# Order of the gather matmuls and of the first weight load within the routed experts of a mixture-of-experts stage

## The chip, the cores and the metric

One Trainium2 chip, eight cores. The batch has eight sequences and each core computes one of them on its own; nothing is exchanged. The time is that of the slowest core in microseconds (us) on the device.

## What is computed

One transformer layer with adaptive layer norm: an attention block, then the feed-forward block below, each with a residual. Only the feed-forward block is touched.

```python
def _L0_ffn_ref(hidden_states, gate_w, sh_gate, sh_up, sh_down, rt_gate, rt_up, rt_down):
    ...
    x = hidden_states.reshape(-1, h)
    logits = x @ gate_w
    top_val = jnp.max(logits, axis=-1, keepdims=True)
    top_id = jnp.argmax(logits, axis=-1)
    score = jax.nn.sigmoid(top_val)
    xs = x * score
    g = jnp.einsum('th,ehi->eti', xs, rt_gate)
    u = jnp.einsum('th,ehi->eti', xs, rt_up)
    act = jax.nn.silu(g) * u
    y = jnp.einsum('eti,eih->eth', act, rt_down)
    onehot = jax.nn.one_hot(top_id, E, dtype=x.dtype)
    routed = jnp.einsum('eth,te->th', y, onehot)
    shared = _swiglu(x, sh_gate, sh_up, sh_down)
    return (shared + routed).reshape(b, s, h)
```

Per core there are 2048 tokens of width 1024, eight experts (E) and an inner width of 2048. Weights come as float32.

## The kernel before, in words

The kernel gives each token to its best expert alone. Up to 384 tokens (`CAP`, three blocks `NSC` of 128) go to each expert. Tokens are collected and put back by matmuls with 0/1 matrices: `Pg_buf` (scaled by the score) gathers, `Ps_buf` scatters.

Each expert e goes through these stages, all on the same engines in program order:

- **Gate and up** (from line 962): 16 steps over `ic`, chunks of 128 of the inner width. `load_guchunk` brings a chunk of `rtg` into `wg_ch[ic % 2]` and of `rtu` into `wu_ch[ic % 2]`, two buffers each, one step ahead. TensorE does 8 + 8 matmuls (line 175) on the gathered tokens `Xg`; ScalarE and VectorE turn them into `act_sl`.
- **Build** (line 993 on): `build_Ps(e)` (lines 917 to 937) makes the scatter matrix by TensorE, ScalarE and VectorE; then `build_Pg(e + 1)` (line 904) makes the next gather matrix by 16 VectorE instructions.
- **Down** (loop around line 1006): 16 steps over `ic`. `load_wd` brings 128 rows of `rtd` into `wd_bf[ic % 2]`, also two buffers; six matmuls add into the six banks pp[2] to pp[7]. In between stand the eight **gather units** of the next expert (`gather_unit(e + 1, dc)`, 16 matmuls of 128x384 of line 175 and one VectorE copy to `Xg`, line 951): one behind every second step. The last expert has none.
- **Yg** (line 1021): six VectorE copies of the six banks, behind any copy to `Xg` on that engine.
- **Scatter** (line 1036 ends it): 32 groups of three matmuls, each followed by one VectorE update of `Xf`.

All weight loads are issued by GpSimd (POOL) and cast to bf16 on the way. POOL works through its queue in program order; a load waits there until TensorE has read the buffer that it overwrites. The loads of chunk 0 of gate and up stand at the head of each expert (lines 960 and 961), chunk 1 right behind them. Nothing plans the order: it is the order in which the Python code emits, and `Emit.op` adds the waits that the buffers need.

Of the kernel before, what the change touches and what calls it, by code (L numbers as in the profile page):

```python
# [104 lines left out]
def build_nc(S=2048, NH=16, IDIM=2048, E=8, CAP=384, debug_stop=None):  # L105
# [3 lines left out]
    IC = IDIM // 128  # L109
# [6 lines left out]
    def din(name, shape, dtype=F32):  # L116
        return nc.dram_tensor(name, shape, dtype, kind="ExternalInput")
# [12 lines left out]
    rtg_h = din("rtg", [E, 2, DC, 128, IH])  # L130
    rtu_h = din("rtu", [E, 2, DC, 128, IH])
# [22 lines left out]
    with em.ctx:  # L154
        ctx = em.ctx

        def sbuf(name, shape, dtype=F32, stack=None):
            return (stack or ctx).enter_context(
                nc.sbuf_tensor(name, shape, dtype))
# [5 lines left out]
        def dma(dst_ap, src_ap, writes, reads=(), eng="sync", sem=None):  # L165
            assert sem is not None
            em.op(eng, lambda E, d=dst_ap, s=src_ap: E.dma_start(d, s),  # L167
                  reads=reads, writes=writes, sem=sem, delta=16)

        def mmg(chain, writes, reads):  # L170
            n = len(chain)
            for i, (o, l, r) in enumerate(chain):
                em.op("tensor",
                      lambda E, o=o, l=l, r=r, a=(i == 0), z=(i == n - 1):
                      E.matmul(o, l, r, start=a, stop=z,  # L175
                               skip_group_check=True),
                      reads=(reads if (i == 0 or i == n - 1) else ()),
                      writes=(writes if (i == 0 or i == n - 1) else ()))
# [511 lines left out]
        with ExitStack() as ph4:  # L690
# [19 lines left out]
            def router_tc(tc):  # L710
                for t4 in range(4):
                    tb = tc * 4 + t4
                    if tb >= NB:
# [42 lines left out]
            wg_ch = [sbuf(f"wg_ch{i}", [128, DC * 128], BF16, ph4)  # L756
                     for i in range(2)]
            wu_ch = [sbuf(f"wu_ch{i}", [128, DC * 128], BF16, ph4)
                     for i in range(2)]
            rwg = [Res(), Res()]  # L760
            rwu = [Res(), Res()]
# [58 lines left out]
            def load_guchunk(ppe, prouted, src, dst, rr, ic, csem):  # L820
                hf = ic // (IC // 2)
                cc = (ic % (IC // 2)) * 128
                ap = (src.ap()[ppe, hf] if prouted else src.ap()[hf])
                dma(dst[:].rearrange("p (c n) -> p c n", c=DC),
                    ap.rearrange("c p n -> p c n")[:, :, cc:cc + 128],
                    writes=[rr], eng="gpsimd", sem=csem)
# [74 lines left out]
            def build_Pg(e):  # L901
                for tb in range(NB):
                    em.op("vector",
                          lambda E_, t=tb, e=e, NE=E: E_.tensor_scalar(  # L904
                              Pg_buf[:, t * CAP:t * CAP + CAP],
                              iotaf[:, 0:CAP],
                              rank_f[:, t * NE + e:t * NE + e + 1],
                              score_f[:, t:t + 1],
                              ALU.is_equal, ALU.mult),
                          reads=[rrk, rscf, rconst], writes=[rPg])  # L910
# [46 lines left out]
            for dc in range(DC):  # L957
                gather_unit(0, dc)
            for e in range(E):
                load_guchunk(e, True, rtg_h, wg_ch[0], rwg[0], 0, "dwg0")  # L960
                load_guchunk(e, True, rtu_h, wu_ch[0], rwu[0], 0, "dwu0")
                for ic in range(IC):
                    cb_ = ic % 2
                    if ic + 1 < IC:
                        load_guchunk(e, True, rtg_h, wg_ch[(ic + 1) % 2],
                                     rwg[(ic + 1) % 2], ic + 1,
                                     f"dwg{(ic + 1) % 2}")
                        load_guchunk(e, True, rtu_h, wu_ch[(ic + 1) % 2],
                                     rwu[(ic + 1) % 2], ic + 1,
                                     f"dwu{(ic + 1) % 2}")  # L970
                    pg, pu = pp[2 + (ic % 2)], pp[4 + (ic % 2)]
                    rpg, rpu = rpp[2 + (ic % 2)], rpp[4 + (ic % 2)]
                    mmg([(pg[:, 0:CAP],
                          wg_ch[cb_][:, dc * 128:(dc + 1) * 128],
                          Xg[:, dc * CAP:(dc + 1) * CAP])
                         for dc in range(DC)],
                        writes=[rpg], reads=[rwg[cb_], rXg])
                    mmg([(pu[:, 0:CAP],
                          wu_ch[cb_][:, dc * 128:(dc + 1) * 128],
                          Xg[:, dc * CAP:(dc + 1) * CAP])  # L980
                         for dc in range(DC)],
                        writes=[rpu], reads=[rwu[cb_], rXg])
                    em.op("scalar",
                          lambda E, p=pg, i=ic: E.activation(  # L984
                              silu_sb[i % 2][:, 0:CAP], p[:, 0:CAP],
                              AF.Silu),
                          reads=[rpg], writes=[rsilu[ic % 2]])
                    em.op("vector",
                          lambda E, i=ic, p=pu: E.tensor_mul(  # L989
                              act_sl[:, i * 512:i * 512 + CAP],  # L990
                              silu_sb[i % 2][:, 0:CAP], p[:, 0:CAP]),
                          reads=[rsilu[ic % 2], rpu], writes=[ract])
                build_Ps(e)
                if e + 1 < E:
                    build_Pg(e + 1)
                gu = list(range(DC)) if e + 1 < E else []
                gui = 0
                for ic in range(IC):
                    load_wd(e, True, rtd_h, ic)
                    for sc in range(NSC):  # L1000
                        for dh in range(2):
                            k = sc * 2 + dh
                            em.op("tensor",
                                  lambda E, i=ic, s2=sc, d2=dh, b2=ic % 2,
                                  k=k, a=(ic == 0), z=(ic == IC - 1):
                                  E.matmul(  # L1006
                                      pp[2 + k][:],
                                      act_sl[:, i * 512 + s2 * 128:
                                             i * 512 + (s2 + 1) * 128],
                                      wd_bf[b2][:, d2 * 512:(d2 + 1) * 512],  # L1010
                                      start=a, stop=z,
                                      skip_group_check=True),
                                  reads=[rwd[ic % 2], ract],
                                  writes=([rpp[2 + k]] if ic in (0, IC - 1)
                                          else ()))
                    while gui < len(gu) * (ic + 1) // IC:
                        gather_unit(e + 1, gu[gui])
                        gui += 1
                for k in range(NSC * 2):
                    em.op("vector",  # L1020
                          lambda E_, k=k: E_.tensor_copy(  # L1021
                              Yg[:, k * 512:(k + 1) * 512], pp[2 + k][:]),
                          reads=[rpp[2 + k]], writes=[rYg])
                for dc in range(DC):
                    for tc in range(NTC):
                        k = 6 + (dc * NTC + tc) % 2
                        chain = [(pp[k][:],
                                  Yg[:, sc * D + dc * 128:
                                     sc * D + (dc + 1) * 128],
                                  Ps_buf[:, (sc * NTC + tc) * 512:  # L1030
                                         (sc * NTC + tc + 1) * 512])
                                 for sc in range(NSC)]
                        mmg(chain, writes=[rpp[k]], reads=[rYg, rPs])
                        em.op("vector",
                              lambda E_, d=dc, t=tc, k=k:
                              E_.scalar_tensor_tensor(  # L1036
                                  Xf[d][:, t * 512:(t + 1) * 512],
                                  pp[k][:],
                                  mod_sb[:, GB + d:GB + d + 1],
                                  Xf[d][:, t * 512:(t + 1) * 512],  # L1040
                                  ALU.mult, ALU.add),
                              reads=[rpp[k], rmod, rXf[dc]],
                              writes=[rXf[dc]])
# [90 lines left out]
```

How the kernel before makes its waits and increments, by code:

```python
        def run(E, fn=fn, final=tuple(final), sem=sem, delta=delta):  # L71
            for (s, v) in final:
                E.wait_ge(sems[s], v)
            ins = fn(E)
            ins.then_inc(sems[sem], delta)
            return ins
# [28 lines left out]
def build_nc(S=2048, NH=16, IDIM=2048, E=8, CAP=384, debug_stop=None):  # L105
# [299 lines left out]
        def _dump_and_exit(aps_res):  # L405
            rout = Res()
            for (dst, src, rr, eng) in aps_res:
                dma(dst, src, writes=[rout], reads=[rr], eng=eng, sem="so")
            fin = em.cnt["so"]
            em.raw("sync", lambda E: E.wait_ge(em.sems["so"], fin))
            em.flush()
# [629 lines left out]
                                  ALU.mult, ALU.add),  # L1041
                              reads=[rpp[k], rmod, rXf[dc]],
                              writes=[rXf[dc]])
            em.flush()
        rout = Res()
        for dc in range(DC):
            dma(y_h.ap()[dc * 128:(dc + 1) * 128, :], Xf[dc][:],
                writes=[rout], reads=[rXf[dc]], sem="so")
        fin = em.cnt["so"]
        em.raw("sync", lambda E: E.wait_ge(em.sems["so"], fin))
        em.flush()
    return nc
```

## Time and profile before

| | us |
|---|---|
| median of 2 runs | 3915.04 (3908.28 to 3921.79) |
| profiled execution | 3910.82 |
| its span on the slowest core (core 3) | 3909.3 |
| spans of the eight cores | 3862.2 to 3909.3 |
| TensorE busy in that span | 2721.3 (70%) |

The profiled execution is 1.5 us longer than its span, and 4.2 us below the median. The profile gives for each engine its instructions with start and duration, and for each idle time what ended it (the releaser). TensorE's instructions are pipelined, so the distance between starts tells more than the durations.

### The profile page before, as it was taken

Reading aid. Unit: us, or ns where it says so; the run is one execution under the profiler, and the core shown is the slowest. Engines: PE = TensorE matmul, PEld = TensorE weight load, DVE = VectorE, ACT = ScalarE, POOL = GpSimd, SP = SyncE. Lnnn points to the kernel's source line nnn. Section 1 sums busy time; section 2 is a strip of 40 time slices with the busy share of each in tenths; the row PEclk is TensorE's granted clock in tenths of the full one; section 3 lists DMA queues with packets and bytes.
Section 4 is the critical chain, followed back from the end, with each engine's and each line's share of the span. In section 5 each row is a group of like instructions: output and inputs, shape, how many; then the busy total and the mean of one; then the engine's idle time right before and its main releaser. Section 6 shows DMA issues by size and latency. Waiting matters only on the chain.

```text
span 3909.3 us, 36235 instructions; the slowest of 8 cores (3862.2 to 3909.3 us)
## 1 busy us (share of the span) xinstructions
PE 2721.3 (70%) x11400; PEld 1135.4 (29%) x11400; DVE 970.3 (25%) x1892; ACT 630.9 (16%) x1007; POOL 468.1 (12%) x614
## 2 busy tenths in 40 slices
PE   2972888888788888617767756676666767675854
PEld 2950322222222222203222323232222222232321
DVE  0024221221221211451110132233232423232312
ACT  0032233333333332321000000000001010100000
POOL 0000000000000000003222312121212121212120
PEclk9985877878887865858999979898989889898987
DMA  4402300000000000009979937483838383838483
GB/s 156 161 33 18 34 6 3 9 3 6 9 3 1 1 1 0 1 1 100 99 85 99 103 44 73 57 81 49 81 49 81 49 81 49 82 48 86 51 90 108
DMA packets 466446, 204.25 MB, mean 52 GB/s; under 512 B 438231, under 2 KB 438490, under 8 KB 463194
## 3 DMA queue, kind: packets, MB, share of 16 engines
q0 software_dynamic: 462368, 184.60, 41.1%
q1 hardware_dynamic: 3898, 17.32, 1.3%
q8 instruction: 104, 1.70, 0.2%
q14 instruction: 76, 0.62, 0.1%
HBM read 352.89 MB, written 8.39 MB: 92 GB/s over the span
## 4 chain that ended last, share of the span: by engine, by line
DMA 22%; PE 19%; DVE 7%; issue 5%; ACT 0%; DVEq 0%; POOL 0%; POOLq 0%; ACTq 0%
PE pp L175 12%; DMA wu_ch<-rtu 7%; DMA wd_bf<-rtd 6%; DMA wd_bf<-shd 4%; DMA wu_ch<-shu 3%; PE pp L1006 3%; PE pp L869 2%; DVE Xf L1036 2%; DVE Ps_buf L937 2%; DMA wg_ch<-rtg 2%; DVE Pg_buf L904 2%; DMA wg_ch<-shg 1%; DVE Yg L1021 1%; PE pp L917 1%; PE pp L930 0%
## 5 line engine op out<-in xcount | busy, mean ns | idle before, releaser
L550 PE MATMUL s_ps<-Qall,Kall 64*128 64x512 bf16 (+3 forms) x640 | 256.1, 414 | 122.7 <-DVE s_ps L559 94.0
L593 PE MATMUL z_ps<-PT,Vb 128*64 128x512 bf16 (+3 forms) x640 | 284.3, 444 | 58.9 <-ACT PT L567 40.9
L984 ACT ACTIVATE silu<-pp 128x384 f32<-128x384 f32 x128 | 62.9, 491 | 1392.0 <-PE pp L175 1392.0
L175 PE MATMUL pp<-Ps_buf,Yg 128*128 128x512 bf16 x768 | 235.3, 404 | 67.5 <-DVE Yg L1021 41.0
L605 PE MATMUL l_ps<-PT,onescol_s 128*1 128x512 bf16 (+3 forms) x640 | 263.8, 412 | 0.0
L175 PE MATMUL pp<-Xg,wu_ch 128*128 128x384 bf16 x1024 | 195.5, 335 | 96.3 <-DMA wu_ch<-rtu 95.2
L1006 PE MATMUL pp<-wd_bf,act_sl 128*128 128x512 bf16 x768 | 204.7, 411 | 74.9 <-DMA wd_bf<-rtd 74.4
L175 PE MATMUL pp<-Xg,wg_ch 128*128 128x384 bf16 x1024 | 194.9, 335 | 70.8 <-DMA wg_ch<-rtg 69.0
L175 PE MATMUL pp<-Pg_buf,h2tm 128*128 128x384 bf16 x1024 | 191.6, 345 | 61.2 <-DVE Pg_buf L904 61.2
L567 ACT ACTIVATE PT<-s_ps 128x1024 bf16<-128x1024 f32 x192 | 191.2, 1013 | 231.9 <-PE s_ps L550 230.5
L244 PE MATMUL mod_ps<-c_sil,wmodb 128*128 128x1 f32 x768 | 164.0, 352 | 76.2 <-ACT c_sil L225 76.2
L1036 DVE SCALAR_TENSOR_TENSOR Xf<-pp,mod_sb,Xf 128x512 f32<-128x512 f32 x256 | 192.0, 751 | 78.5 <-PE pp L175 70.2
L869 PE MATMUL pp<-act_sl,wd_bf 128*128 128x512 bf16 x512 | 132.9, 410 | 98.9 <-DMA wd_bf<-shd 97.8
L989 DVE TENSOR_TENSOR act_sl<-silu,pp 128x384 bf16<-128x384 f32 x128 | 70.9, 554 | 474.9 <-PE pp L175 444.3
L244 PEld LDWEIGHTS mod_ps<-c_sil,wmodb 128*128 128x128 f32 x768 | 163.9, 333 | 76.2 <-issue 76.2
L167 POOL DMA_DIRECT2D wg_ch<-rtg x128 | 112.4, 878 | 521.1 <-PE pp L175 503.2
L577 ACT ACTIVATE PT<-s_ps 128x512 bf16<-128x512 f32 (+3 forms) x256 | 110.5, 437 | 300.1 <-DVE s_ps L559 208.3
L175 PEld LDWEIGHTS pp<-Xg,wu_ch 128*128 128x128 bf16 x1024 | 95.2, 99 | 191.6 <-issue 141.4
L550 PEld LDWEIGHTS s_ps<-Qall,Kall 64*128 64x128 bf16 x640 | 60.0, 95 | 301.0 <-issue 290.3
L175 PEld LDWEIGHTS pp<-Pg_buf,h2tm 128*128 128x128 bf16 x1024 | 104.6, 103 | 145.9 <-issue 81.6
L175 PE MATMUL pp<-Hb,wu_ch 128*128 128x512 bf16 x512 | 122.9, 383 | 31.5 <-DMA wu_ch<-shu 31.0
L175 PEld LDWEIGHTS pp<-Xg,wg_ch 128*128 128x128 bf16 x1024 | 95.2, 99 | 164.3 <-issue 114.4
(142 smaller groups left out, 2608.8 us busy)
## 6 DMA issues: line engine op xcount, KB each, us to landing
wg_ch<-rtg POOLq DMA_DIRECT2D x128, 256.0 KB, 6.3
wu_ch<-rtu POOLq DMA_DIRECT2D x128, 256.0 KB, 6.5
wd_bf<-rtd POOLq DMA_DIRECT2D x128, 256.0 KB, 4.2
wmodb<-wmod POOLq DMA_DIRECT2D x8, 3072.0 KB, 13.2
wg_ch<-shg POOLq DMA_DIRECT2D x64, 256.0 KB, 6.3
wu_ch<-shu POOLq DMA_DIRECT2D x64, 256.0 KB, 6.2
wd_bf<-shd POOLq DMA_DIRECT2D x64, 256.0 KB, 4.1
Xf<-x SPq DMA_DIRECT2D x8, 1024.0 KB
```

The costliest lines, as they stand in the source:

```text
L167: em.op(eng, lambda E, d=dst_ap, s=src_ap: E.dma_start(d, s), reads=reads, writes=writes, sem=sem, delta=16)
L175: E.matmul(o, l, r, start=a, stop=z, skip_group_check=True),
L244: lambda E, b=b, j=j, dc=dc: E.matmul(mod_ps[:, j:j + 1], wmod_bf[b][:, j * 128:(j + 1) * 128], c_sil[:, dc:dc + 1], start=(dc == 0 and j ...
L550: E.matmul(p[:, o + c:o + 512], Kall[bb][h, k * 128:(k + 1) * 128], Qall[bb][h, q], start=True, stop=True, skip_group_check=True),
L567: lambda E, p=sb_, t=pt: E.activation(t[:, 0:1024], p[:, 0:1024], AF.Exp),
L577: E.activation(t[:, o + c:o + 512], p[:, o + c:o + 512], AF.Exp),
L593: E.matmul(z_ps[zz, c:512], Vb[bb][:, k * 128 + h * 64: k * 128 + h * 64 + 64], t[:, o + c:o + 512], start=a, stop=z, skip_group_check=True),
L605: E.matmul(l_ps[:, c:512], onescol[:], t[:, o + c:o + 512], start=a, stop=z, skip_group_check=True),
L869: E.matmul(pp[d][:], wd_bf[b2][:, d * 128:(d + 1) * 128], act_sl[:, i * 512:(i + 1) * 512], start=a, stop=z, skip_group_check=True),
L904: lambda E_, t=tb, e=e, NE=E: E_.tensor_scalar(Pg_buf[:, t * CAP:t * CAP + CAP], iotaf[:, 0:CAP], rank_f[:, t * NE + e:t * NE + e + 1], sc ...
L1006: E.matmul(pp[2 + k][:], act_sl[:, i * 512 + s2 * 128: i * 512 + (s2 + 1) * 128], wd_bf[b2][:, d2 * 512:(d2 + 1) * 512], start=a, stop=z, ...
L1036: E_.scalar_tensor_tensor(Xf[d][:, t * 512:(t + 1) * 512], pp[k][:], mod_sb[:, GB + d:GB + d + 1], Xf[d][:, t * 512:(t + 1) * 512], ALU.mu ...
```

## The change

The gather units are emitted twice as densely: one behind each of the down steps 0 to 7, and none behind steps 8 to 15. The loads of chunk 0 of the next expert move from the head of that expert to behind down step 12, that is between the loads of down chunks 12 and 13. Chunk 1 stays where it was. Nothing is added or removed but by these moves; the last expert's down stage stays as it is.

```diff
@@ -957,8 +957,9 @@
             for dc in range(DC):
                 gather_unit(0, dc)
             for e in range(E):
-                load_guchunk(e, True, rtg_h, wg_ch[0], rwg[0], 0, "dwg0")
-                load_guchunk(e, True, rtu_h, wu_ch[0], rwu[0], 0, "dwu0")
+                if e == 0:
+                    load_guchunk(e, True, rtg_h, wg_ch[0], rwg[0], 0, "dwg0")
+                    load_guchunk(e, True, rtu_h, wu_ch[0], rwu[0], 0, "dwu0")
                 for ic in range(IC):
                     cb_ = ic % 2
                     if ic + 1 < IC:
@@ -1013,9 +1014,14 @@
                                   reads=[rwd[ic % 2], ract],
                                   writes=([rpp[2 + k]] if ic in (0, IC - 1)
                                           else ()))
-                    while gui < len(gu) * (ic + 1) // IC:
+                    while gui < min(len(gu), len(gu) * (ic + 1) * 2 // IC):
                         gather_unit(e + 1, gu[gui])
                         gui += 1
+                    if ic == IC - 4 and e + 1 < E:
+                        load_guchunk(e + 1, True, rtg_h, wg_ch[0], rwg[0],
+                                     0, "dwg0")
+                        load_guchunk(e + 1, True, rtu_h, wu_ch[0], rwu[0],
+                                     0, "dwu0")
```

On TensorE, the down stage of an expert (line 1006 is the down matmul; `pp<-Pg_buf,h2tm` is a gather unit; `pp<-Ps_buf,Yg` the scatter) reads before:

```order
L930 MATMUL pp<-rank_row,onesh_s 128x512 x4
L1006 MATMUL pp<-wd_bf,act_sl 128x512 x12
L175 MATMUL pp<-Pg_buf,h2tm 128x384 x16
L1006 MATMUL pp<-wd_bf,act_sl 128x512 x12
L175 MATMUL pp<-Pg_buf,h2tm 128x384 x16
```

and its end, before:

```order
L1006 MATMUL pp<-wd_bf,act_sl 128x512 x12
L175 MATMUL pp<-Pg_buf,h2tm 128x384 x16
L175 MATMUL pp<-Ps_buf,Yg 128x512 x96
```

The same stage of the changed kernel begins with (line 1006 is 1007 there):

```order
L930 MATMUL pp<-rank_row,onesh_s 128x512 x4
L1007 MATMUL pp<-wd_bf,act_sl 128x512 x6
L175 MATMUL pp<-Pg_buf,h2tm 128x384 x16
L1007 MATMUL pp<-wd_bf,act_sl 128x512 x6
L175 MATMUL pp<-Pg_buf,h2tm 128x384 x16
```

and ends with:

```order
L1007 MATMUL pp<-wd_bf,act_sl 128x512 x6
L175 MATMUL pp<-Pg_buf,h2tm 128x384 x16
L1007 MATMUL pp<-wd_bf,act_sl 128x512 x48
L175 MATMUL pp<-Ps_buf,Yg 128x512 x96
```

One down step (six matmuls) now stands ahead of the first gather unit where there were two, and eight down steps (48 matmuls) follow each other without a gather unit.

On POOL, the queue around the end of an expert before (each row is one load or a run of loads, `rtd` the down weights):

```order
L167 DMA wd_bf<-rtd 128x1024 x16
L167 DMA wg_ch<-rtg 128x8x128
L167 DMA wu_ch<-rtu 128x8x128
L167 DMA wg_ch<-rtg 128x8x128
L167 DMA wu_ch<-rtu 128x8x128
```

and now:

```order
L167 DMA wd_bf<-rtd 128x1024 x13
L167 DMA wg_ch<-rtg 128x8x128
L167 DMA wu_ch<-rtu 128x8x128
L167 DMA wd_bf<-rtd 128x1024 x3
L167 DMA wg_ch<-rtg 128x8x128
L167 DMA wu_ch<-rtu 128x8x128
```

The pair of chunk 0 has moved ahead of the last three down loads; the pair of chunk 1 still stands behind the last one.

## Rows read from the trace of the kernel before

**Rows 1.** The page's first line: the span of the profiled core and of all cores.

```profile
span 3909.3 us, 36235 instructions; the slowest of 8 cores (3862.2 to 3909.3 us)
```

**Rows 2.** Windows: stretch, us, busy us by engine (instructions), granted clock, DMA share, GB/s.

```profile
3620.40:3671.60 51.20, 38.31 (x197) 18.53 (x196) 8.52 (x14) 0.00 (x0) 9.88 (x16) 0.97 0.65 83
...
3704.00:3769.50 65.50, 45.89 (x257) 22.97 (x255) 9.06 (x16) 7.86 (x16) 25.59 (x30) 1.00 1.27 121
...
3789.30:3842.80 53.50, 28.33 (x98) 9.37 (x98) 6.41 (x9) 0.00 (x0) 7.41 (x14) 0.85 0.51 69
```

**Rows 3.** Waits of TensorE from 2440 us on: total us, times, longest.

```profile
PE pp L1006 <- DMA wd_bf<-rtd: 74.4, 66, 3.1
```

**Rows 4.** Timeline of TensorE, down stage of expert 6: start, us, [idle before <-releaser].

```profile
3603.16 4.89 PE L1006 MATMUL pp<-wd_bf,act_sl 128*128 128x512 bf16 x12
3615.31 5.28 PE L175 MATMUL pp<-Pg_buf,h2tm 128*128 128x384 bf16 x16 [7.25 <-DVE Pg_buf L904]
3620.38 3.15 PE L1006 MATMUL pp<-wd_bf,act_sl 128*128 128x512 bf16 x12
...
3629.20 1.46 PE L1006 MATMUL pp<-wd_bf,act_sl 128*128 128x512 bf16 x6 [1.11 <-DMA wd_bf<-rtd]
3630.50 2.76 PE L175 MATMUL pp<-Pg_buf,h2tm 128*128 128x384 bf16 x16
3633.10 1.46 PE L1006 MATMUL pp<-wd_bf,act_sl 128*128 128x512 bf16 x6
...
3663.41 2.76 PE L175 MATMUL pp<-Pg_buf,h2tm 128*128 128x384 bf16 x16
3671.62 4.88 PE L175 MATMUL pp<-Ps_buf,Yg 128*128 128x512 bf16 x12 [5.45 <-DVE Yg L1021]
```

**Rows 5.** The same timeline, expert 0: first gather unit and first scatter.

```profile
2479.70 5.12 PE L175 MATMUL pp<-Pg_buf,h2tm 128*128 128x384 bf16 x16 [7.72 <-DVE Pg_buf L904]
...
2535.23 4.76 PE L175 MATMUL pp<-Ps_buf,Yg 128*128 128x512 bf16 x12 [5.45 <-DVE Yg L1021]
```

**Rows 6.** The same timeline, expert 7, which has no gather units: steps 2 and 15, scatter.

```profile
3796.38 1.45 PE L1006 MATMUL pp<-wd_bf,act_sl 128*128 128x512 bf16 x6 [1.80 <-DMA wd_bf<-rtd]
...
3837.18 2.72 PE L1006 MATMUL pp<-wd_bf,act_sl 128*128 128x512 bf16 x6 [3.12 <-DMA wd_bf<-rtd]
3842.79 4.69 PE L175 MATMUL pp<-Ps_buf,Yg 128*128 128x512 bf16 x12 [2.89 <-DVE Yg L1021]
```

**Rows 7.** Timeline of POOL: issues at the end of expert 6, and one in expert 7.

```profile
3657.46 0.53 POOL L167 DMA_DIRECT2D wd_bf<-rtd  x1 [1.61 <-PE pp L175]
3657.98 0.90 POOL L167 DMA_DIRECT2D wg_ch<-rtg  x1
3658.86 0.90 POOL L167 DMA_DIRECT2D wu_ch<-rtu  x1
...
3705.98 0.88 POOL L167 DMA_DIRECT2D wg_ch<-rtg  x1 [44.47 <-PE pp L175]
...
3798.66 0.53 POOL L167 DMA_DIRECT2D wd_bf<-rtd  x1 [3.02 <-PE pp L1006]
```

**Rows 8.** Issue to landing: all wd loads; expert 7's; its first two; wu of 3658.86.

```profile
DMA to landing us min/median/max: 3.5/4.2/8.6
...
DMA to landing us min/median/max: 3.6/3.9/4.5
...
DMA to landing us min/median/max: 6.0/6.4/6.7
...
DMA to landing us min/median/max: 6.0/6.0/6.0
```

**Rows 9.** Timeline of VectorE, the copies to Yg of expert 6.

```profile
3666.82 4.66 DVE L1021 CAST Yg<-pp 128x512 bf16<-128x512 f32 x6
```

**Rows 10.** Windows of expert 7's 16 down steps on core 5 and core 2, columns as in rows 2.

```profile
3782.80:3838.00 55.20, 36.67 (x97) 11.23 (x96) 3.20 (x5) 0.00 (x0) 7.40 (x14) 0.65 0.47 67
...
3775.90:3823.00 47.10, 25.61 (x97) 8.88 (x96) 3.08 (x5) 0.00 (x0) 7.40 (x14) 0.95 0.54 78
```

## The prediction

> **What bounds the kernel now.** I read the page for the span [rows 1], then windows by stage, then TensorE's waits, then the timeline of the stage that the change touches. The span of core 3, the slowest, is 3909.3 us and the execution took 3910.82. The three stages of an expert look unlike each other [rows 2]: gate and up has the DMA engines full (share 1.27) and TensorE busy 46 of 65.5 us; the down stage with gather units has TensorE busy 38 of 51 us at DMA share 0.65; the down stage of the last expert, without gather units, has it busy only 28 of 53.5 us. So in the down stage neither engine is full. What holds it is the round trip of a `wd_bf` buffer: step, then issue, then landing, then the step after next. Together TensorE waits 74.4 us for down weights from 2440 us on [rows 3], in 66 pieces.
>
> The timeline of expert 6 shows the shape [rows 4]. Steps 0 and 1 run at 3603.16, then TensorE sits idle 7.25 us for VectorE's `Pg_buf`. The first gather unit starts at 3615.31; call this point P. Everything later depends on P, and P is set by VectorE building `Ps_buf` and `Pg_buf`, which the change does not touch. The scatter starts at 3671.62; call this S. P to S is 56.3 us here and 55.5 in expert 0 [rows 5]; all seven experts that have gather units lie between 55.1 and 56.3. The forecast is a sum for P to S after the change.
>
> The pieces, at the full clock: a down step takes 1.30 us from start to start (3629.20 to 3630.50), a gather unit 2.60 (3630.50 to 3633.10), and the first gather unit, at the lower clock behind the idle time, 5.07 (3615.31 to 3620.38) [rows 4]. The round trip: in expert 7 step 2 starts at 3796.38 [rows 6], the load into its buffer is issued 2.28 later at 3798.66 [rows 7], and it lands after 3.9 in the median [rows 8]: 6.2 us from step k to step k+2, at least. TensorE's own work over two steps is 2.6 us bare, 5.2 with one gather unit, 7.8 with two. Bare, the round trip decides and TensorE idles 3.6 us a pair; with one it idles about 1; with two it idles nothing, and 1.6 us of cover goes to waste. That is the change: instead of eight pairs with one unit each, four with two and four with none.
>
> **Part 1, the gather units.** From P: first gather unit 5.07. Then seven steps (1 to 7) and seven gather units, 7 x (1.30 + 2.60) = 27.3. No load holds them, since a buffer comes round every 7.8 us against 6.2. Step 8 starts at P + 32.4. Step 1 is part of this: it used to run ahead of P, in the idle time, and now stands behind the gather unit that waits for VectorE, and the issue of down load 3 waits for it.
>
> Steps 8 to 15 are bare. Expert 7 has exactly this pattern, and its steps 2 to 15 took 3837.18 - 3796.38 = 40.8 us for 13 distances, 3.14 each [rows 6]. So step 15 starts 7 x 3.14 = 22.0 later, at P + 54.4.
>
> From step 15 to the scatter expert 7 took 3842.79 - 3837.18 = 5.6 us [rows 6]: TensorE waits only for the six copies to `Yg`, 4.66 us together [rows 9]. Before, the last gather unit stood in between, and its copy to `Xg` ahead of those six on VectorE: step 15 starts at 3663.41 - 1.30 = 3662.11, S at 3671.62, 9.5 us [rows 4]. This 3.9 us is the gain of the change, and it is in the sum since I put 5.6 there. What is late next is the copies themselves.
>
> **Part 2, the moved chunk 0.** As to waiting nothing is gained: in expert 6 the pair was issued at 3657.98 and 3658.86 [rows 7] and the second landed 6.0 us later [rows 8], at 3664.9, while POOL's next issue, which waits for the first use of that chunk, comes at 3705.98 [rows 7]. It was some 39 us early already, under the scatter. If that cover were gone it would cost up to one landing, 6 us an expert; but it stays, for chunk 1 too, which is still issued behind down load 15 and has the whole scatter.
>
> It costs something. The two issues, 0.9 us each, fit in POOL's idle time between down loads 12 and 13, some 3 us. They wait for nothing but their own earlier transfers. But their data stand ahead of down load 13. From the issue of load 12: the `wu_ch` load is issued at 1.4 (3657.46 to 3658.86) and lands 6.0 later, at 7.4. Two down loads issued 0.56 apart right behind chunk loads landed after 6.0 and 6.7 [rows 8], that is 1.3 apart; so load 13 lands at about 8.7. Alone it would land at 3.1 + 3.9 = 7.0. That makes 1.7 us, and since step 15 hangs on step 13 it reaches the end. Bounds: nothing, if the transfers share the engines; and 4.1 us, the whole time that one pair of chunks takes where DMA is full (65.5 / 16 [rows 2]). I take 1.7.
>
> **Sum.** 5.07 + 27.3 + 22.0 + 1.7 + 5.6 = 61.7 us from P to S against 56.3 before: 5.4 us more for each expert. The scatter and the gate stage follow unchanged. Seven experts: 7 x 5.4 = 38 us, 3910.8 + 38 = 3949. The median of the runs shown is 4.2 us over the profiled execution, so the predicted median is 3953, 1.0% above before. Bounds of the sum: bare steps at the quickest landing seen, 3.5 [rows 8], give (2.28 + 3.5) / 2 = 2.89 a step, 20.2 for seven; with no cost of part 2 that is 58.2, +1.9 an expert, +13 us. The other end is the clock, below.
>
> **Rivals.** *The clock falls in the bare half.* The granted clock of expert 7's bare steps was 0.65 on core 5 and 0.95 on core 2, in windows of 55.2 and 47.1 us for the same 16 steps [rows 10]. So the sparse pattern can hold TensorE at the lower level (1.2 GHz), and then it costs 8.1 us in 13 to 15 distances, 0.6 a step, through the step's own length in the round trip. Seven distances: 4.4 us an expert, 31 us in all, 3949 + 31 = 3980, as a median 3984. Against it: the other half of the stage is now dense, and cores 3 and 2 kept the full clock most of the way. The slowest core sets the time, which speaks for part of it.
>
> On this the Trainium skill (TensorE: Matmul & The Clock Gate, HAM oscillation) says that short bursts of matmuls between waits for DMA can keep the array throttled. The trace agrees on core 5 and not on core 2.
>
> *The bare half is quicker than its model, and the change comes out not slower.* The place is the landing of down loads in steps 10 to 15. P to S is 56.3 again when 7 x (2.28 + L) / 2 = 56.3 - 32.4 - 5.6 = 18.3, that is at a landing L of 2.95 us and with no cost of part 2. Half a microsecond below that point the sum is 54.6, -1.7 an expert, -12 us: 3899, as a median 3903. At the very end stands TensorE's own pace, 7 x 1.30 = 9.1 and 47.1 in all, -64 us. Against it: no wd load of this trace landed under 3.5, and expert 7's, which had the DMA engines to themselves, took 3.9 [rows 8].
>
> The Trainium skill (DMA: Bandwidth & Descriptors, Anatomy of one DMA) gives a transfer about 2.0 us plus bytes at 436 GB/s; as an estimate that is 2.6 us for the 256 KB written or 3.2 for the 512 KB read, which would be this rival or near it. The rows have 3.9 for the same transfer and decide.
>
> *The moved loads hold more than one step.* If load 13 waits for the whole pair (4.1 us) and load 14 behind it is late as well, part 2 costs 5 to 6 us instead of 1.7, and with half of the clock's price each expert loses some 11 us: 78 us, 3989. For it: eight cores load at once, and one down load took 8.6 us [rows 8]. Against it: load 14 is issued only after step 12, when the pair is nearly through.
>
> **How the numbers follow.** The forecast 0.66, the clock rival 0.20, not slower 0.06, the moved loads 0.08. The first two and the third case all lie within 2% (78 us), which is about what a measurement of this kernel tells from no change; only the last reaches over it. Faster by over 2% 0.02, within 0.90, slower by over 2% 0.08. The range goes from 3925 (+13 with a little below the median's 3928) to 3985 (the clock rival in full).
>
> **What would show it.** In the changed trace, steps 0 to 7 with TensorE waiting nowhere for `wd_bf` after P; steps 8 to 15 at 3.0 to 3.3 us apart; the wait for `Yg` near 3 us instead of 5.45; down load 13 landing in 5 to 6 us; the total wait for `wd_bf` up from 74 to about 7 x 14 + 22 = 120 us; P to S of 60 to 63 us. It is wrong if steps 8 to 15 come under 2.7 us apart, if P itself moves, or if the gate stage (65.5 us) gets shorter because of chunk 0.

## The result and the profile after

The changed kernel took 3968.77 us in the median of 11 runs (3958.57 to 4011.12), the kernel before 3925.96 in the runs on the same chips. The ratio is 1.0118, with a 95% interval from 1.0084 to 1.0152. A second measurement, given below, found 1.0184 (1.0139 to 1.0229). All ratios here leave out the executions in which one die ran longer at a lower granted clock, and of the four executions of the second measurement two remain. So the change costs some 1% to 2% (the two intervals together run from 0.8% to 2.3%): slower, 16 us above the forecast 3953, and inside the range.

The page of the profiled execution begins so (core 5, the slowest; to hold against [rows 1]):

```profile
span 3990.1 us, 36284 instructions; the slowest of 8 cores (3915.3 to 3990.1 us)
```

One profiled execution against another says little, since executions of one kernel spread by 50 us and more. The stage itself is read more sharply: it occurs seven times on each of eight cores. First the timeline of TensorE after the change, core 3, down stage of expert 0 (line 1007 is the old 1006; to hold against [rows 4, 5]):

```profile
2459.16 2.74 PE L1007 MATMUL pp<-wd_bf,act_sl 128*128 128x512 bf16 x6
2471.22 5.28 PE L175 MATMUL pp<-Pg_buf,h2tm 128*128 128x384 bf16 x16 [9.32 <-DVE Pg_buf L904]
2476.30 1.85 PE L1007 MATMUL pp<-wd_bf,act_sl 128*128 128x512 bf16 x6
...
2501.36 2.76 PE L175 MATMUL pp<-Pg_buf,h2tm 128*128 128x384 bf16 x16
2503.96 1.46 PE L1007 MATMUL pp<-wd_bf,act_sl 128*128 128x512 bf16 x6
2506.25 1.46 PE L1007 MATMUL pp<-wd_bf,act_sl 128*128 128x512 bf16 x6 [0.84 <-DMA wd_bf<-rtd]
2510.03 1.58 PE L1007 MATMUL pp<-wd_bf,act_sl 128*128 128x512 bf16 x6 [2.32 <-DMA wd_bf<-rtd]
2512.78 2.72 PE L1007 MATMUL pp<-wd_bf,act_sl 128*128 128x512 bf16 x6 [1.18 <-DMA wd_bf<-rtd]
2516.68 2.72 PE L1007 MATMUL pp<-wd_bf,act_sl 128*128 128x512 bf16 x6 [1.18 <-DMA wd_bf<-rtd]
2522.74 5.28 PE L1007 MATMUL pp<-wd_bf,act_sl 128*128 128x512 bf16 x12 [3.34 <-DMA wd_bf<-rtd]
2530.66 1.73 PE L1007 MATMUL pp<-wd_bf,act_sl 128*128 128x512 bf16 x6 [2.64 <-DMA wd_bf<-rtd]
2536.06 9.23 PE L175 MATMUL pp<-Ps_buf,Yg 128*128 128x512 bf16 x24 [3.67 <-DVE Yg L1027]
```

Three things are to be seen. The dense half (2476.30 to 2503.96) has no wait at all. In the bare half from 2503.96 every step but the first waits for its load or stands behind one that did, and from the fourth to the seventh a step of six matmuls takes some 2.7 us instead of 1.46: the lower clock. The last two rows hold the gain: step 15 starts at 2530.66 and the scatter at 2536.06, 5.4 us later and not 9.5.

The windows of these two halves (columns as in [rows 2]) show the clock beside it, 0.91 and 0.67:

```profile
2471.22:2503.96 32.74, 32.74 (x170) 17.48 (x171) 3.90 (x7) 0.00 (x0) 3.70 (x7) 0.91 0.36 50
2503.96:2536.06 32.10, 16.94 (x51) 5.17 (x49) 4.71 (x7) 0.00 (x0) 6.77 (x10) 0.67 0.75 89
```

And the waits of TensorE on the same core, from 2440 us on (total us, times, longest); the first row answers to [rows 3]:

```profile
PE pp L1007 <- DMA wd_bf<-rtd: 102.4, 53, 4.1
...
PE pp L175 <- DVE Pg_buf L904: 65.2, 7, 9.3
PE pp L175 <- DVE Yg L1027: 28.4, 8, 4.3
```

The last two of these read before, on the same core:

```profile
PE pp L175 <- DVE Pg_buf L904: 51.4, 7, 7.7
PE pp L175 <- DVE Yg L1021: 41.0, 8, 5.5
```

The wait for down weights went from 74.4 to 102.4 us; each wait for `Pg_buf` from some 7.3 to 9.3, which is step 1 that no longer fills it; the wait for `Yg` fell from 41.0 to 28.4.

From here on P to S is the mean over experts 0 to 6 and eight cores of the distance from the first gather matmul that waited for `Pg_buf` to the first scatter matmul, 56 readings of a profiled execution for each kernel, good to about 0.1 us in the mean:

| kernel | P to S, us | P to step 8 | step 8 to 15 | step 15 to S | ratio to before (95%) |
|---|---|---|---|---|---|
| before | 54.8 | | | 9.5 | |
| changed | 63.6 | 32.2 | 25.9 | 5.5 | 1.0118 (1.0084 to 1.0152) |
| changed, again | 63.1 | 31.9 | 25.7 | 5.5 | 1.0184 (1.0139 to 1.0229) |

(P to step 8 is the start of the last gather unit plus its 2.60 us; step 15 to S is read on the six cores whose records are complete; step 8 to 15 is the rest.) The gate stage is 67.7 us in the mean before and 68.0 after, the scatter 32.5 in both, and from the first down step to P it is 12.0 in both: the time went into P to S, 8.3 to 8.8 us an expert, and nowhere else. Seven times that is 58 to 62 us or 1.5 to 1.6%, between the two measurements.

### The profile page after: what moved, and what is told of

It reads as the page before. It is cut to its first block, busy times and chain, and to the rows that moved or that the text cites. A ratio compares the mean times of both kernels' runs of the same rounds, so it can differ in the third digit from the quotient of the medians.

```text
span 3990.1 us, 36284 instructions; the slowest of 8 cores (3915.3 to 3990.1 us)
## 1 busy us (share of the span) xinstructions
PE 2813.1 (71%) x11400; PEld 1151.8 (29%) x11400; DVE 971.4 (24%) x1892; ACT 630.4 (16%) x1007; POOL 468.2 (12%) x614
## 4 chain that ended last, share of the span: by engine, by line
PE 21%; DMA 19%; DVE 6%; issue 5%; ACT 0%; POOL 0%; DVEq 0%; POOLq 0%; ACTq 0%
PE pp L175 14%; DMA wu_ch<-rtu 7%; DMA wd_bf<-rtd 4%; PE pp L1007 4%; DMA wd_bf<-shd 4%; DMA wu_ch<-shu 2%; PE pp L869 2%; DVE Xf L1042 2%; DVE Ps_buf L937 2%; DVE Pg_buf L904 2%; DMA wg_ch<-shg 1%; DMA wg_ch<-rtg 1%; PE pp L917 1%; DVE Yg L1027 1%; PE pp L930 0%
## 5 line engine op out<-in xcount | busy, mean ns | idle before, releaser
L550 PE MATMUL s_ps<-Qall,Kall 64*128 64x512 bf16 (+3 forms) x640 | 265.9, 429 | 122.1 <-DVE s_ps L559 93.5
L593 PE MATMUL z_ps<-PT,Vb 128*64 128x512 bf16 (+3 forms) x640 | 299.7, 468 | 56.7 <-ACT PT L567 39.3
L1007 PE MATMUL pp<-wd_bf,act_sl 128*128 128x512 bf16 x768 | 245.8, 471 | 111.3 <-DMA wd_bf<-rtd 111.2
L605 PE MATMUL l_ps<-PT,onescol_s 128*1 128x512 bf16 (+3 forms) x640 | 277.2, 433 | 0.0
L1007 PEld LDWEIGHTS pp<-wd_bf,act_sl 128*128 128x128 bf16 x768 | 81.7, 112 | 254.6 <-issue 213.6
L550 PEld LDWEIGHTS s_ps<-Qall,Kall 64*128 64x128 bf16 x640 | 60.5, 96 | 308.2 <-issue 298.9
L167 POOL DMA_DIRECT2D wd_bf<-rtd x128 | 68.5, 536 | 662.0 <-PE pp L1007 409.4
```

The costliest lines, as they stand in the source:

```text
L550: E.matmul(p[:, o + c:o + 512], Kall[bb][h, k * 128:(k + 1) * 128], Qall[bb][h, q], start=True, stop=True, skip_group_check=True),
L593: E.matmul(z_ps[zz, c:512], Vb[bb][:, k * 128 + h * 64: k * 128 + h * 64 + 64], t[:, o + c:o + 512], start=a, stop=z, skip_group_check=True),
L605: E.matmul(l_ps[:, c:512], onescol[:], t[:, o + c:o + 512], start=a, stop=z, skip_group_check=True),
L1007: E.matmul(pp[2 + k][:], act_sl[:, i * 512 + s2 * 128: i * 512 + (s2 + 1) * 128], wd_bf[b2][:, d2 * 512:(d2 + 1) * 512], start=a, stop=z, ...
```

## The experiments

Theory A is the forecast: two buffers' round trip holds the bare half, and the moved loads delay down load 13. All ratios are to the kernel before on the same chip.

**The two parts apart.** The first kernel has only the packed gather units and is called gather-only below. Against the changed kernel it lacks:

```diff
-                    if ic == IC - 4 and e + 1 < E:
-                        load_guchunk(e + 1, True, rtg_h, wg_ch[0], ...)
-                        load_guchunk(e + 1, True, rtu_h, wu_ch[0], ...)
```

(and the loads back at the head of the expert). What was expected:

> Only the gather units are packed into steps 0 to 7; the loads of chunk 0 stay at the head of the expert. P to S (first gather unit to scatter, mean over seven experts and eight cores) is 54.8 us before and 63.6 after. Theory A (the bare half runs at the round trip of two buffers, and the moved loads cost some 1.7 us an expert): P to S about 62, the time some 12 us under the changed kernel, +0.9% on before. Rival B (the moved loads hold several steps): P to S 60 or less, and more than half of the loss gone, +0.5% or less.

Measured: 1.0104 (1.0072 to 1.0136), P to S 60.5 us. That is 5.7 more than before, and 3.1 less than the changed kernel. The number lies between the two theories: the moved loads cost more than 1.7, but not most of the loss.

The second, called loads-only, has only the moved loads, `while gui < len(gu) * (ic + 1) // IC` as before:

> Only the loads of chunk 0 move (behind step 12); the gather units stay behind every second step. Theory A: P to S 54.8 + 1.7 = 56.5 us, +12 us in all, +0.3%. Rival B: +4 us or more an expert, P to S 59 or more, +0.7%. If the prefetch were worth something, the gate stage (67.7 us in the mean before) would be shorter; I expect it unchanged to 0.5 us.

Measured: 1.0059 (1.0040 to 1.0078), P to S 57.9, 3.1 more than before; 5.7 + 3.1 = 8.8, so the parts add up to the 63.6 of the changed kernel. Again between the theories. Where 3.1 comes from is seen in TensorE's timeline of this kernel, core 3, steps 12 to 15 of one expert (the last row holds 14 and 15):

```profile
3463.32 1.46 PE L1007 MATMUL pp<-wd_bf,act_sl 128*128 128x512 bf16 x6
3468.03 1.54 PE L1007 MATMUL pp<-wd_bf,act_sl 128*128 128x512 bf16 x6 [3.25 <-DMA wd_bf<-rtd]
3469.36 4.40 PE L175 MATMUL pp<-Pg_buf,h2tm 128*128 128x384 bf16 x16
3473.60 2.90 PE L1007 MATMUL pp<-wd_bf,act_sl 128*128 128x512 bf16 x12
```

Step 13 waits 3.25 us where such waits were about 1, and then the gather unit behind it takes 4.40 us instead of 2.76: the longer wait is followed by a spell at the lower clock. The load that step 13 waited for, read on its own:

```profile
L167 POOL DMA_DIRECT2D wd_bf<-rtd x1: 557/557/557, 3461.4 to 3461.4; - x1
...
DMA to landing us min/median/max: 6.5/6.5/6.5
```

In the mean of experts 0 to 6 and eight cores (56 loads) load 13 lands 6.6 us after its issue in this kernel and 6.8 in the changed one, against 4.2 before. Counted from the issue of load 12 it lands at 9.2 here, against 6.7 before: 2.5 of the 3.1 us. No other load of steps 11 to 15 is late by more than 0.6 us in this kernel. The gate stage is no shorter either: 68.3 us in the mean here, 69.0 in the gather-only kernel and 67.7 before. This mean lies anywhere between 65.8 and 69.5 in the profiled executions of all kernels here, without an order by where the loads stand, so it would not show a gain of a microsecond. But there was no wait that the prefetch could have ended: before the change chunk 0 landed 39 us ahead of its first use already, after it 47.

**Where the loads stand.** The pair behind step 3 instead of 12, `if ic == 3 and e + 1 < E`:

> The changed kernel, but the loads of chunk 0 stand behind step 3 instead of step 12, in the dense half, where a buffer comes round every 7.8 us and the round trip needs 6.2. Theory A: the slack of 1.6 us swallows the 1.7 us, so the time and P to S equal those of the gather-only kernel within 0.5 us an expert. Rival B (the loads cost the same wherever they stand in the down stage): P to S as in the changed kernel, 63.6.

Measured: 1.0103 (1.0056 to 1.0151), P to S 60.3, that of the gather-only kernel (60.5). In the dense half the same two loads are free: down load 4 behind them lands 5.2 us after its issue in the mean instead of 3.8, and TensorE loses under 0.2 us by it. POOL's timeline shows the loads there, with the next down load 2.51 us behind the second and the one after it on its usual beat of 3.9:

```profile
2478.23 0.90 POOL L167 DMA_DIRECT2D wg_ch<-rtg  x1
2479.11 0.91 POOL L167 DMA_DIRECT2D wu_ch<-rtu  x1
2481.62 0.56 POOL L167 DMA_DIRECT2D wd_bf<-rtd  x1 [1.60 <-PE pp L175]
2485.51 0.54 POOL L167 DMA_DIRECT2D wd_bf<-rtd  x1 [3.34 <-PE pp L175]
```

**Half of the loads.** The kernel before with only the gate half of chunk 0 behind step 12 (and no longer at the head of experts 1 to 7):

```diff
+                    if ic == IC - 4 and e + 1 < E:
+                        load_guchunk(e + 1, True, rtg_h, wg_ch[0], ...)
```

> The kernel before with only the gate half of chunk 0 moved behind step 12; its up half stays at the head. The whole pair cost 3.1 us an expert (P to S 57.9 against 54.8). If load 13 queues behind the moved bytes, half of them cost about half: P to S 56.0 to 56.6. If it is the mere presence of a load there (POOL's issue, a semaphore), it costs nearly the whole: 57.5 or more; if up to the slack nothing shows, 55.3 or less.

Measured: 0.9997 (0.9960 to 1.0033), P to S 55.1. All of the expected cases but the last are wrong: half of the bytes cost 0.3 us (0.1 on cores 4 to 7 taken alone, 54.7 against 54.6), not half of 3.1. The mean landings explain it. The gate load is issued 0.5 us behind down load 12 and lands 5.2 later, at 5.7; load 13 is issued at 2.2 and lands 4.9 later, at 7.1, hardly after the 6.7 of before. With the pair, in the loads-only kernel, the up load lands at 1.4 + 6.45 = 7.9 and load 13 at 2.5 + 6.6 = 9.2. In both it lands 1.3 to 1.4 behind its last predecessor, the distance that the prediction took from the rows. In these two kernels the load is late by as much as that point lies behind its own landing of before, and not by a share of the bytes.

**The clock.** The gather-only kernel with filler behind each bare step, that is eight matmuls whose result nobody reads:

```diff
+                    if ic >= IC // 2 and e + 1 < E:
+                        mmg([(pp[0][:, 0:CAP], identb[:],
+                              act_sl[:, ic * 512:ic * 512 + CAP])
+                             for _ in range(8)],
+                            writes=[rpp[0]], reads=[ract])
```

> The gather-only kernel, with eight matmuls of 128x384 added behind each bare step 8 to 15 into a bank that nobody reads then: they fill TensorE's wait (1.3 us of about 1.8) and change no other order. If the lower granted clock in the bare half is part of the loss (rival: clock), P to S falls by about 2 us under the gather-only kernel although TensorE has more to do, and the granted clock there rises to 0.95 or more. If the clock costs nothing (theory A without it), P to S stays or rises by up to 1 us.

Measured: 1.0079 (1.0057 to 1.0102), P to S 59.0 against 60.5. TensorE has 64 matmuls more to do in the stage and is through 1.5 us sooner. (The two ratios alone, 1.0079 and 1.0104, can't be told apart; the 56 readings each of P to S can.) In the windows of the bare half on core 3, without filler and with it, the granted clock is 0.77 and 1.00:

```profile
2504.36:2533.72 29.36, 17.08 (x51) 5.33 (x48) 4.71 (x7) 0.00 (x0) 6.70 (x10) 0.77 0.79 97
```

```profile
2512.33:2538.99 26.66, 22.05 (x114) 10.38 (x112) 4.71 (x7) 0.00 (x0) 6.70 (x10) 1.00 0.86 106
```

Over all cores with complete records a down matmul of steps 10 to 15 (a step's length by six) took 0.34 us in the mean without filler, 0.24 with it, and 0.37 in the changed kernel; in steps 2 to 8 it is 0.24 to 0.25 in all of them. With the clock held, steps 8 to 15 are (59.0 - 31.9 - 5.3) / 7 = 3.11 us apart, against the round trip (2.28 + 3.9) / 2 = 3.09 of the prediction. That its two terms give nearly this is in part luck: in steps 10 to 15 of this kernel a load is issued 2.0 us after the step that frees its buffer and lands 4.1 later, and the step that reads it starts 0.2 behind that. The timeline of the filler kernel, core 3, shows what is left of the waits:

```profile
2518.45 1.46 PE L1006 MATMUL pp<-wd_bf,act_sl 128*128 128x512 bf16 x6 [0.60 <-DMA wd_bf<-rtd]
2519.74 1.46 PE L175 MATMUL pp<-act_sl,identb_s 128*128 128x384 bf16 x8
2521.26 1.46 PE L1006 MATMUL pp<-wd_bf,act_sl 128*128 128x512 bf16 x6
2522.55 1.46 PE L175 MATMUL pp<-act_sl,identb_s 128*128 128x384 bf16 x8
2524.67 1.46 PE L1006 MATMUL pp<-wd_bf,act_sl 128*128 128x512 bf16 x6 [0.65 <-DMA wd_bf<-rtd]
```

2518.45 to 2524.67 is 6.2 us for two steps.

The same filler in the changed kernel:

> The changed kernel with the same filler matmuls behind steps 8 to 15 as before, so that the granted clock stays up and the moved loads' cost stands alone. Gather-only with filler had P to S 59.0, the changed kernel 63.6. If the pair costs only the later landing of load 13 (mean 6.5 us after issue instead of 4.2), P to S is 59.0 + 2.2 = 61.2 us; if it is 62 or more, the landing of one load does not account for it and other loads are late too.

Measured: 1.0112 (1.0069 to 1.0156), P to S 61.8, 2.8 above gather-only with filler. So 61.2 was a little low and 62 is not reached. The landing of load 13 accounts for it: in the mean of 56 loads it lands 6.7 us after its issue here, against 4.0 in gather-only with filler, and counted from the issue of load 12 at 9.65 against 6.93, 2.7 later.

**More buffers.** If it is the round trip of two buffers, four must cure it. The two more lie in rows of `Hb` that nobody reads any more:

```diff
+            wdx = [wd_bf[0][:], wd_bf[1][:], Hb[0][:, 0:D], Hb[1][:, 0:D]]
+            rwdx = [rwd[0], rwd[1], rHb[0], rHb[1]]
...
+                    dma(wdx[ic % 4], src[ic * 128:(ic + 1) * 128, :],
+                        writes=[rwdx[ic % 4]], eng="gpsimd",
+                        sem=f"dwd{ic % 4}")
```

With the order of before:

> The kernel before with four buffers for the down weights of the routed experts instead of two (the two more lie in the rows of Hb that nobody reads by then); order of work as before. Theory A (the down stage is held by the round trip of a buffer, 2.28 + 3.9 us for two steps): with four buffers it is TensorE's own pace, P to S = 4.6 + 14 x 1.30 + 6 x 2.60 + 8.3 = 46.7 us instead of 54.8, and some 15 us in the last expert: about 70 us, -1.8%. Rival (the transfers' own rate holds the stage, as in gate and up): less than half of that, P to S over 50 us.

Measured: 0.9870 (0.9771 to 0.9969), P to S 47.4, no wait for a down load in it. The expected 46.7 was met within a microsecond; cores 0 to 3 have 46.6 and cores 4 to 7, at a mean clock of 0.81 against 0.84, 48.1. TensorE's timeline, core 3, has a pair of steps and a gather unit at every 5.19 us (2477.57 to 2498.32 is four of them), TensorE's own 5.2:

```profile
2477.57 2.75 PE L1014 MATMUL pp<-wd_bf,act_sl 128*128 128x512 bf16 x12
...
2487.95 2.75 PE L1014 MATMUL pp<-wd_bf,act_sl 128*128 128x512 bf16 x12
...
2498.32 2.75 PE L1014 MATMUL pp<-wd_bf,act_sl 128*128 128x512 bf16 x12
```

With the packed gather units and the loads at the head:

> The gather-only kernel with four buffers. Theory A: the round trip per step is (2.28 + 3.9) / 4 = 1.55 us in the bare half, so P to S = 4.6 + 7 x 3.9 + 7 x 1.5 + 5.5 = 48 us against 60.5 with two buffers, and the packed order costs no more than 2 us an expert against the spread order with four buffers. Rival (transfer rate): eight bare steps in a row want a load each 1.3 us, more than the engines bring; P to S over 52 us.

Measured: 0.9831 (0.9783 to 0.9879), P to S 49.4. The packed order that cost 5.7 us with two buffers costs 2.0 with four (2.8 on cores 0 to 3 alone), and the two ratios can't be told apart. In its bare half TensorE still waits 2.3 us an expert for down loads.

The whole change with four buffers:

> The changed kernel (packed gather units, chunk 0 behind step 12) with four buffers. The moved pair cost 3.1 us an expert with two buffers. Theory A (load 13 queues behind the pair, and with two buffers nothing is left to cover it): with four buffers load 13 is issued some two steps before it is needed, and P to S lies within 1 us of the 49.4 of the packed order with four buffers. Rival: it costs 2 us or more there too (51.4 or more), as eight bare steps leave no slack for any delay.

Measured: 0.9908 (0.9880 to 0.9936), P to S 53.2. The expectation of theory A, that two more buffers absorb the moved pair, fell here: the pair costs 3.8 us, more than with two buffers. POOL's timeline shows that load 13 is no longer held back by its buffer but comes at once behind the pair:

```profile
2497.90 0.53 POOL L167 DMA_DIRECT2D wd_bf<-rtd  x1 [3.37 <-PE pp L1015]
2498.42 0.91 POOL L167 DMA_DIRECT2D wg_ch<-rtg  x1
2499.31 0.90 POOL L167 DMA_DIRECT2D wu_ch<-rtu  x1
2500.18 0.58 POOL L167 DMA_DIRECT2D wd_bf<-rtd  x1
```

and TensorE, whose bare steps start 1.3 us apart while nothing holds them, is through step 12 long before it lands (the two rows are steps 12 and 13):

```profile
2501.88 1.46 PE L1015 MATMUL pp<-wd_bf,act_sl 128*128 128x512 bf16 x6 [0.64 <-DMA wd_bf<-rtd]
2506.95 2.72 PE L1015 MATMUL pp<-wd_bf,act_sl 128*128 128x512 bf16 x6 [3.62 <-DMA wd_bf<-rtd]
```

Loads 13, 14 and 15, issued one behind another, land 1.3 us apart in the mean, which is also TensorE's own bare step. The four buffers hid the latency of one load; they didn't hide the pair put in front of a run that goes at the transfers' own pace.

**What was good in the change, alone.** The kernel before with the last two gather units behind steps 12 and 14 instead of 13 and 15:

```diff
-                    while gui < len(gu) * (ic + 1) // IC:
+                    while gui < (len(gu) * (ic + 1) // IC if ic < 12 else
+                                 (7 if ic < 14 else len(gu)) if gu else 0):
```

> The kernel before with the last gather unit moved from behind step 15 to behind step 14 and the one before it from behind step 13 to behind step 12; two buffers, loads of chunk 0 at the head. It takes only what was good in the change: the copies to Yg follow step 15 at once. Theory A: step 15 to S falls from 9.6 to 5.5 us and the steps lose up to 1 us of cover: P to S about 51.5 to 52.5, 7 x 2.8 = 20 us, -0.5%. Rival (the gain of the tail is given back by a wait of step 15 for its load): P to S 54 or more.

Measured: 0.9946 (0.9918 to 0.9974), P to S 51.8, as expected, step 15 to the scatter 5.6. On core 3 step 15 starts at 2539.32 and the scatter at 2545.04:

```profile
2536.72 2.76 PE L175 MATMUL pp<-Pg_buf,h2tm 128*128 128x384 bf16 x16
2539.32 1.46 PE L1006 MATMUL pp<-wd_bf,act_sl 128*128 128x512 bf16 x6
...
2545.04 4.57 PE L175 MATMUL pp<-Ps_buf,Yg 128*128 128x512 bf16 x12 [4.26 <-DVE Yg L1022]
```

Both together:

> Both of what helped, together: gather units behind steps 1, 3, 5, 7, 9, 11, 12 and 14, four buffers for the down weights, loads of chunk 0 at the head. Four buffers alone gave P to S 47.4 us (from 54.8), the earlier last unit alone 51.8. Theory A: with four buffers no step needs cover, so the tail's 3.9 to 4.1 us come on top: P to S 43.5, against before 7 x 11.3 + 20 (last expert) = 99 us, -2.5%. Rival: the last steps, closer together at the end, wait for their loads again, or VectorE's copies hold the end; P to S 46 or more, -2.0% or less.

Measured: 0.9792 (0.9756 to 0.9828), 3812.71 us against 3900.61, the lowest ratio of all, though its interval touches that of gather-only with four buffers. P to S is 45.5, not 43.5 (45.2 on cores 0 to 3). The expectation was worked out wrongly: with four buffers there is no wait that a gather unit could cover, so moving it ahead of step 15 saves only what `Yg` waited for its copy to `Xg`, and its own 2.6 us stay. The sum is 4.6 (the first gather unit in the mean) + 13 x 1.30 + 7 x 2.60 + 5.5 = 45.2.

Last, the changed kernel again:

> The changed kernel as it is, once more, beside the others on one chip. Theory A, by the sum of the parts (gather order +5.7 us, moved loads +3.1 us an expert): P to S 63.6 again and 7 x 8.8 = 62 us, +1.6% on before, at the upper end of the first measurement's interval (0.84% to 1.52%). Rival: part of the 62 us is made up elsewhere and the ratio stays near 1.2%.

Measured: 1.0184 (1.0139 to 1.0229), P to S 63.1. The 1.6% of theory A lies in this interval and just above the first one; the rival's 1.2% lies outside it.

## Why the prediction was right, and where its sizes were off

The sign, the place and the mechanism held. The stage lost over half as much again as was forecast (8.3 to 8.8 us an expert and not 5.4). That the median came out only 16 us above 3953 was in part luck: the medians of the first measurement lie 43 us apart, where the stage gives 58 to 62. Point by point, in the prediction's own steps:

- **P does not move, and the gate stage gains nothing.** Right: the first gather unit still waits for `Pg_buf`, and gate stays at 68 us.
- **Front half, 7 x (1.30 + 2.60) = 27.3 us, no wait.** Right: 32.2 - 4.6 = 27.6, and no wait in it. The first gather unit took 4.6 us in the mean, not 5.07. The dense half wastes cover.
- **Bare half, 7 x 3.14 = 22.0.** Mis-sized by 1.1 at the clock: gather-only took 60.5 - 31.9 - 5.5 = 23.1. At the full clock it is 21.8 (with filler). The clock rival is thus partly true, everywhere and not on single cores: 1.5 us an expert by the filler pair 60.5 and 59.0, and about as much between 63.1 to 63.6 and 61.8 in the changed kernel. The 22.0 held only part of it, as expert 7's steps did.
- **The tail, 5.6 instead of 9.5.** Right: 5.5 against 9.5.
- **The moved loads, 1.7.** Mis-sized: 2.8 with the clock held, 3.1 without. Both of its terms were off. The prediction had load 13 land 8.7 us after load 12's issue; it lands at 9.2 in the loads-only kernel and at 9.7 in the changed one (9.5 the second time), because the up load ahead of it took 6.5 to 6.8 us and not 6.0. And it let load 13 alone be issued 3.1 behind load 12, the mean step. In truth the steps come in unequal pairs, and before the change load 13 goes out 2.4 behind and lands at 6.7, not 7.0. That makes 2.5 to 3.0 us of later landing. In the loads-only kernel some 0.6 is left over; the clock behind the long wait, shown in one place above, is the likely rest, but no run holds it alone.
- **The base.** P to S before was taken as 56.3, expert 6 of core 3. The mean over cores and experts is 54.8. These 1.5 us made the loss look smaller, and are the largest single part of the difference between the 5.4 us forecast and the 8.3 to 8.8 found. Seven times the difference of some 3 us is what separates the 38 us forecast from the 58 to 62 found.
- **The quicker bare half** did not come about: 3.11 us a step at the full clock, and landings of 4.1 us, a little above expert 7's 3.9.
- **Moved loads that hold more than one step** did not come about either; load 14 lands in 4.4 us in the loads-only kernel, against 3.8.

Of the signs named ahead, the dense half without a wait, and the wait for `Yg` of 3.67 us, came as said. Steps 8 to 15 were forecast 3.0 to 3.3 us apart and are 3.7 (3.3 in gather-only), load 13 to land in 5 to 6 us and takes 6.8, P to S 60 to 63 us and is 63.1 to 63.6. The total wait for down weights was forecast at about 120 us and is 102 on core 3: part of the loss is no wait but matmuls at the lower clock. None of the three signs of a wrong mechanism was seen.

The granted clock of the bare half was between 0.73 and 0.84 on each of the eight cores of the changed kernel, and 0.97 to 1.00 with the gaps filled. On this the Trainium skill (TensorE: Matmul & The Clock Gate, HAM oscillation) says that short bursts of matmuls between waits for DMA keep throttling the array again. The runs agree with it on all cores (0.34 us a matmul in gather-only against 0.24 with the gaps filled), though never with the whole stage throttled.

## What to carry to other kernels

Other work placed between steps that wait for a round trip is worth most when it is spread so that each round trip is just covered: two units in one gap cover it once, and the bare gap is paid in full. A load put ahead of others on one queue should go where the buffers turn round slower than their round trip; in the tight stretch even loads that nobody waits for are paid by those behind them, once they land late enough. And before a sum is set against "before", take that "before" as a mean over all repeats of the stage, not from the instance whose rows are at hand.

## What the runs showed that was not expected

Adding 64 matmuls that compute nothing to each expert made the stage 1.5 us shorter, since the array kept its full clock (1.00 against 0.77 in the bare half). And the cost of loads ahead of another did not go by their bytes: one load of 256 KB cost 0.3 us an expert, two cost 3.1. And the last gather unit ahead of step 15, the part of the change that was good, is worth 3.0 us an expert when it is taken alone.
